# Four scatter stages, four product banks, and a last layer whose input part is worked out ahead of the attention

## What is computed

```python
x = x + einsum('bct,bcd->bdt', x, w0[subject])          # per-sequence 32x32 mix
x = x + einsum('bct,bcd->bdt', x, w1[condition])        # per-sequence 32x32 mix
x = x + attention(x, Wq, Wk, Wv, Wo, k_blocks, v_blocks, tables, lens)
x = x + (x @ W.T + (x @ A[a].T @ Bm[a].T) * scaling[a])  # a: adapter of the sequence
```

## Time and profile before

| what | us |
| --- | --- |
| median of three runs | 499.41 |
| lowest, highest | 495.37, 501.82 |
| the profiled execution | 497.69 |
| its span in the trace | 495.9 |
| TensorE busy in it | 382.6 |
| VectorE busy | 345.0 |
| ScalarE busy | 266.1 |
| GpSimd (POOL) busy | 107.7 |

### The profile page before, as it was taken

One profiled execution on the slowest core, in us unless ns is written; L12 is line 12 of the kernel. 1 busy time (PEld: TensorE's weight loads), 2 busy tenths in 40 slices (PEclk: granted clock), 3 DMA queues, 4 the chain that ended last, 5 costly groups with the idle time before them and its releaser, 6 DMA issues.

```text
span 495.9 us, 16985 instructions
## 1 busy us (share of the span) xinstructions
PE 382.6 (77%) x6190; PEld 283.8 (57%) x6190; DVE 345.0 (70%) x1017; ACT 266.1 (54%) x977; POOL 107.7 (22%) x178
## 2 busy tenths in 40 slices
PE   1753777888875006969879999999899999987996
PEld 0342534444442004757767777777777777776785
DVE  6994277898889805647656677677777777765782
ACT  3302555666665105545645766666766676654662
POOL 5300043333334620211211221211211221220000
PEclk9855798999999555799989999999999999998999
DMA  3999122222212066788877768867878969875200
GB/s 111 386 399 385 44 79 74 73 78 72 78 55 81 21 140 169 154 163 172 191 191 168 163 169 171 169 153 165 186 173 160 191 173 162 180 188 128 71 24 23
DMA packets 68866, 73.57 MB, mean 148 GB/s; under 512 B 18190, under 2 KB 65326, under 8 KB 66528
## 3 DMA queue, kind: packets, MB, share of 16 engines
q1 hardware_dynamic: 61968, 39.38, 33.9%
q0 software_dynamic: 6864, 33.72, 25.0%
HBM read 70.83 MB, written 26.21 MB: 196 GB/s over the span
## 4 chain that ended last, share of the span: by engine, by line
PE 32%; DMA 18%; ACT 9%; issue 5%; DVE 1%; SPq 1%; ACTq 0%; DVEq 0%; POOLq 0%
PE probT_bank L1123 6%; ACT rope L608 6%; PE out_bank L1147 5%; DMA kvbuf<-new_scratch,winidx 5%; PE score_banks L1084 4%; PE keys_bank L1066 3%; DMA window<-value_scratch 3%; DMA value_scratch<-kvbuf 3%; PE score_banks L1079 3%; ACT window L599 3%; PE out_bank L1134 3%; DMA out<-early 3%; DMA kvbuf<-in_kv,winidx 2%; PE out_bank L1148 2%; PE out_bank L1141 2%
## 5 line engine op out<-in xcount | busy, mean ns | idle before, releaser
L608 ACT ACTIVATE rope<-score_banks,negm 128x176 f32<-128x176 f32 x256 | 102.0, 414 | 4.2 <-DVE negm L886 4.0
L886 DVE TENSOR_REDUCE negm<-score_banks 128x2 f32<-128x352 f32 x128 | 61.0, 518 | 35.1 <-PE score_banks L1084 34.4
L896 DVE TENSOR_SCALAR rope<-rope,rinv 128x176 f32<-128x176 f32 x256 | 69.6, 314 | 4.6
L624 ACT COPY early<-probT_bank 128x128 f32<-128x128 f32 x64 | 17.0, 266 | 88.4 <-PE probT_bank L1123 88.4
L1011 PE MATMUL probT_bank<-wts,x2T 128*128 128x512 f32 x128 | 63.1, 617 | 1.8 <-DVE early L732 1.8
L433 POOL DMA_INDIRECT new_scratch<-stage,rowidx x32 | 36.5, 1142 | 111.9 <-DVE stage L757 107.0
L903 DVE COPY rope<-probT_bank 128x512 f32<-128x512 f32 x64 | 44.3, 692 | 18.6 <-PE probT_bank L1103 14.9
L608 ACT ACTIVATION_READ_ACCUMULATOR rope<-score_banks,negm 128x1 f32 x256 | 54.3, 212 | 0.0
L1123 PE MATMUL probT_bank<-rope,window 128*32 128x64 f32 x2048 | 43.8, 226 | 6.3 <-issue 3.4
L599 ACT COPY window<-keys_bank 128x352 f32<-128x352 f32 x60 | 46.7, 779 | 1.5 <-PE keys_bank L1066 1.5
L1066 PE MATMUL keys_bank<-ident,kvbuf 88*128 88x88 f32 x240 | 32.8, 262 | 16.0 <-ACT window L599 13.9
(11 more groups left out here) (179 smaller groups left out, 705.4 us busy)
## 6 DMA issues: line engine op xcount, KB each, us to landing
value_scratch<-kvbuf SPq DMA_DIRECT2D x16, 704.0 KB
window<-value_scratch SPq DMA_DIRECT2D x16, 512.0 KB, 11.6
work<-in_x SPq DMA_DIRECT2D x16, 256.0 KB, 2.7
new_scratch<-window SPq DMA_DIRECT2D x2, 2048.0 KB, 12.0
out<-early SPq DMA_DIRECT2D x32, 128.0 KB, 5.8
window<-value_scratch SPq DMA_DIRECT2D x32, 96.0 KB, 8.6
new_scratch<-kvbuf SPq DMA_DIRECT2D x1, 2048.0 KB, 14.2
wts<-in_weights SPq DMA_DIRECT2D x1, 1280.0 KB, 8.2
```

The costliest lines, as they stand in the source:

```text
L608: ins = a.activation(prob[:, par, P_AT[h]:P_AT[h] + KEYS], psS[:, h, 0:KEYS], ACT.Exp, bias=negm[:, par, h:h + 1], accum_out=sums[:, par, ...
L886: v.tensor_reduce(negm[:, par, 2 * half:2 * half + 2], psS[:, 2 * half:2 * half + 2, 0:KEYS], axis=AX_X, op=ALU.max, negate=True).then_inc ...
L896: ins = v.tensor_scalar(prob[:, par, at], prob[:, par, at], rinv[:, par, h:h + 1], None, ALU.mult)
```

## The change

Seven things change together.

1. The stage has four slots instead of two, with four semaphores; the wait for a scatter looks four tiles back instead of two.
2. `psQKV` has four banks instead of two; `qkv` may be four tiles ahead of `norm`. Two of the banks held the turned indices, so TensorE waits for their copy before `part2(0)`.
3. The work of L868 to L881 on VectorE stands ahead of the tile stage instead of behind it.
4. The last layer is linear, so it is split. In the gap TensorE makes, per tile, x2 times the weights with the identity (kept in `xres` by ScalarE) and the adapter's A times x2 (masked by VectorE into `xa2`).
5. Also in the gap, Wo is multiplied with the last layer's weights and with A (`fused`), and ScalarE keeps the products in `wo` and `woA`.
6. In the attention stage `project` uses these: two matmuls of 128 and two of 256 columns. `adapter` and `add3` are gone, `final` keeps one matmul of three, and `adapt_x2` on VectorE adds `xa2`.
7. `y_out` moves from ScalarE to VectorE, where it adds `xres`, and waits there for the store.

```diff
-        psT, psQKV, psQT = [psS[:, 2], psS[:, 3]], psP, [psK, psZ]
+        psT, psQKV, psQT = [psS[:, 2], psS[:, 3]], psP + [psS[:, 0], psS[:, 1]], [psK, psZ]
...
-        stage = sb("stage", [P, 2, 512])
+        stage = sb("stage", [P, 4, 512])
...
                 for j in range(2):
-                    scatter(2 * pair + j, j)
+                    scatter(2 * pair + j, 2 * (pair % 2) + j)
...
             def value_rows(n, j, i):
                 act.wait_ge(s["vcopy"], n + 1)
-                wait_from(act, s_scat[j], i * 16)
-                a.copy(stage[:, j, 384:512], vnew[:, j, :]).then_inc(s["vrow"], 1)
+                wait_from(act, s_scat[j], i * 8 - 8 * (j // 2))
+                a.copy(stage[:, j, 384:512], vnew[:, j % 2, :]).then_inc(s["vrow"], 1)
...
+            for u in range(2):
+                act.wait_ge(s["fused"], u + 1)
+                a.copy(woA[:, u, :], psP[u][:, 256:384])
+            act.wait_ge(s["fused"], 2)
+            for u in range(2):
+                a.copy(wo[:, u, :], psP[u][:, 0:256]).then_inc(s["fused_kept"], 1)
+            for n in range(TILES):
+                act.wait_ge(s["x2_made"], n + 1)
+                a.copy(xres[:, n, :], psS[:, n % 2, 0:256]).then_inc(s["x2_kept"], 1)
...
-            for j in range(2):
-                sumsq(j, j)
-                norm(j, j)
-            part2(0, True, True)
...
             dve.wait_ge(s["masks"], 2)
...
             ins.then_inc(s["w3_plus_one"], 1)
 
+            for j in range(2):
+                sumsq(j, j)
+                norm(j, j, j)
+            part2(0, 0, True, True)
...
-            def add3(m):
+            def y_out(m, par):
+                dve.wait_ge(s["l3"], m + 1)
+                if not (isinstance(m, int) and m < 2):
+                    dve.wait_ge(s_out[par], (m - par) * 8)
+                v.tensor_tensor(ys[:, par, :], xres[:, bass.ds(m, 1), :].rearrange("p o f -> p (o f)"), psZ[:, 0:256],
+                                ALU.add).then_inc(s["y"], 1)
...
+            def adapt_x2(m):
+                dve.wait_ge(s["xa_part"], m + 1)
+                v.tensor_tensor(xam, xam, xa2[:, bass.ds(m, 1), :].rearrange("p o n -> p (o n)"), ALU.add).then_inc(s["xam"], 1)
...
                 if par == 1 and not (known and m < 1):
                     adapt_in(m - 1)
+                if par == 0 and not (known and m < 2):
+                    y_out(m - 2, (k // 2) % 2)
                 probT_out(c, par)
+                if par == 1 and not (known and m < 1):
+                    adapt_x2(m - 1)
                 if not last:
-                    normalise(c + 1, 1 - par, 0)
-                if par == 0 and not (known and m < 1):
-                    add3(m - 1)
-                if not last:
-                    normalise(c + 1, 1 - par, 1)
+                    for half in range(2):
+                        normalise(c + 1, 1 - par, half)
...
+            for n in range(TILES):
+                dve.wait_ge(s["x2_made"], n + 1)
+                v.tensor_tensor(xa2[:, n, :].rearrange("p (b t) -> p b t", b=SPT),
+                                psS[:, 2 + n % 2, 0:P].rearrange("p (b t) -> p b t", b=SPT),
+                                spread(admask[:, n * SPT:n * SPT + SPT], 2, ROWS), ALU.mult).then_inc(s["xa2_kept"], 1)
...
             def qkv(n, j):
                 pe.wait_ge(s["xte"], n + 1)
-                wait_from(pe, s["norm"], n - 1)
-                wait_from(pe, s["vcopy"], n - 1)
+                wait_from(pe, s["norm"], n - 3)
+                wait_from(pe, s["vcopy"], n - 3)
...
+            for u in range(2):
+                for at, n, w in ((0, 256, w3T), (256, P, laT)):
+                    for f in range(2):
+                        ins = t_.matmul(psP[u][:, at:at + n], wo[:, f, P * u:P * u + P], w[:, f, :], start=(f == 0), stop=(f == 1))
+                ins.then_inc(s["fused"], 1)
+            for n in range(TILES):
+                wait_from(pe, s["x2_kept"], n - 1)
+                wait_from(pe, s["xa2_kept"], n - 1)
+                for f in range(2):
+                    t_.matmul(psS[:, 2 + n % 2, 0:P], laT[:, f, :], xres[:, n, P * f:P * f + P], start=(f == 0), stop=(f == 1))
+                for f in range(2):
+                    ins = t_.matmul(psS[:, n % 2, 0:256], xres[:, n, P * f:P * f + P], w3T[:, f, :], start=(f == 0), stop=(f == 1))
+                ins.then_inc(s["x2_made"], 1)
...
             def project(m):
                 pe.wait_ge(s["ote"], m * 2 + 2)
                 wait_from(pe, s["y"], m)
-                for f in range(2):
-                    for u in range(2):
-                        ins = t_.matmul(psZ[:, P * f:P * f + P], woT[:, u, P * f:P * f + P], oT[:, u, :],
-                                        start=(u == 0), stop=(u == 1))
+                for u in range(2):
+                    t_.matmul(psZ[:, 256:256 + P], woA[:, u, :], oT[:, u, :], start=(u == 0), stop=(u == 1))
+                for u in range(2):
+                    ins = t_.matmul(psZ[:, 0:256], oT[:, u, :], wo[:, u, :], start=(u == 0), stop=False, skip_group_check=True)
                 ins.then_inc(s["wo"], 1)
...
             def final(m):
                 pe.wait_ge(s["xam"], m + 1)
-                for f in range(2):
-                    t_.matmul(psZ[:, 0:256], x3T[:, P * f:P * f + P], w3T[:, f, :], start=(f == 0), stop=False)
-                t_.matmul(psZ[:, 0:256], xam, lbT, start=False, stop=True).then_inc(s["l3"], 1)
+                t_.matmul(psZ[:, 0:256], xam, lbT, start=False, stop=True, skip_group_check=True).then_inc(s["l3"], 1)
...
+            pe.wait_ge(s["fused_kept"], 2)
+            pe.wait_ge(s["x2_kept"], TILES)
+            pe.wait_ge(s["xa2_kept"], TILES)
             scores(0, 0, 0, 0)
```

More of the change, by code:

```diff
@@ L477, in _ @@
                     g.memset(vnat[:, :, :, 1, :], 0.0).then_inc(s["v_zero"], 1)
-            for j in range(2):
-                pool.wait_ge(s_scat[j], 16 * TILES // 2)
+            for j in range(4):
+                pool.wait_ge(s_scat[j], 16 * TILES // 4)
             for grp in range(2):
@@ L553, in qT_out, with part2 @@
                        psQT[j][:, 0:256].rearrange("p (u b t) -> p u b t", u=2, b=SPT)).then_inc(s["qte"], 1)
-            def part2(i, s1, s2, s3, s4):
+            def part2(i, q, s1, s2, s3, s4):
                 if s3:
                     for j in range(2):
-                        value_rows(i * 2 + j, j, i)
+                        value_rows(i * 2 + j, 2 * q + j, i)
                 if s2:
-                    squares(i * 2 + 2, 0)
-                    values(i * 2 + 2, 0)
+                    squares(i * 2 + 2, 2 - 2 * q)
+                    values(i * 2 + 2, 2 - 2 * q)
                 if s4:
@@ L567, in part2 @@
                     root(i * 2 + 2, 0)
-                    squares(i * 2 + 3, 1)
-                    values(i * 2 + 3, 1)
+                    squares(i * 2 + 3, 3 - 2 * q)
+                    values(i * 2 + 3, 3 - 2 * q)
                 if s1:
@@ L625, in heads_out @@
                        headsT.rearrange("p (s u t) -> p u s t", s=2, u=2)).then_inc(s["ote"], 1)
-            def y_out(m, par):
-                act.wait_ge(s["l3"], m + 1)
-                if not (isinstance(m, int) and m < 2):
-                    act.wait_ge(s_out[par], (m - par) * 8)
-                a.copy(ys[:, par, :], psZ[:, 0:256]).then_inc(s["y"], 1)
             def period(o, k):
@@ L640, in period @@
                 units = k % CPG < 2 and not (known and group >= GROUPS)
-                if par == 0 and not (known and m < 2):
-                    y_out(m - 2, (k // 2) % 2)
                 if not first:
@@ L755, in finish, with part2 @@
                 wait_from(dve, s["qt"], n - 1)
-                wait_from(dve, s_scat[j], i * 16)
-                v.tensor_tensor(stage[:, j, 0:384], rc[:, j, :], rs[:, j, :], ALU.add).then_inc(s["roped"], 1)
-            def part2(i, s2, s3):
+                wait_from(dve, s_scat[j], i * 8 - 8 * (j // 2))
+                v.tensor_tensor(stage[:, j, 0:384], rc[:, j % 2, :], rs[:, j % 2, :], ALU.add).then_inc(s["roped"], 1)
+            def part2(i, q, s2, s3):
                 if s3:
@@ L852, in _ @@
             v.tensor_copy(winidx[:].rearrange("p k g -> p (k g)"), turned_wins[0:GR]).then_inc(s["winidx"], 1)
-            for j in range(2):
-                sumsq(j, j)
-                norm(j, j)
-            part2(0, True, True)
-            part2(1, True, True)
-            base = ch.base + ch.n
-            with dve.Fori(2, PAIRS - 1) as i:
-                ch.start(base + (i - 2) * 10)
-                part2(i, True, True)
-                assert ch.n == 10
-            ch.start(base + 10 * (PAIRS - 3))
-            part2(PAIRS - 1, False, True)
             dve.wait_ge(s["masks"], 2)
@@ L881, in _ @@
             ins.then_inc(s["w3_plus_one"], 1)
+            for j in range(2):
+                sumsq(j, j)
+                norm(j, j, j)
+            part2(0, 0, True, True)
```

(24 more changed lines are left out.)

73 lines of the change are left out of this document (34 added, 39 removed).

## The result

The changed kernel takes 519.11 us (median; 517.04 to 522.40) against 500.62 for the kernel before in the same comparison: a ratio of 1.041, with an interval of 1.029 to 1.053. It is slower by about 18 us. Every ratio and interval here compares executions of both kernels in the chip's faster state alone, while a median is over all executions, so a ratio and a quotient of two medians may differ. The forecast was 504, and the range ended at 515. The profiled execution took 521.12 us, its span is 519.3.

What follows compares the result with a forecast made beforehand. VectorE and the scatter loop were taken to bound the tile stage, TensorE and window loads the attention stage. First unit +31.4 us, attention -24.9, sum +6.5 on a profiled 497.7: 504 us, range 493 to 515.

Steps and rivals of the forecast that it cites:

- The mask work, +8.4 on the path: Start of tile stage: mask work on VectorE ahead of the first sum delays everything by the full 8.4 us.
- Pairs 6.29 to 6.14: Tile stage: four stages and banks end the scatter wait, saving 0.15 us a pair; with early pairs -4.5 us together.
- The last scatter 5.80 to 1.0: End of tile stage: without mask work beside it, POOL's last scatter shortens, -4.8 us.
- The gap, +31.4: Between tile and attention stages: TensorE's new work moves the first unit from 184.72 to 216.1 us.
- Rival E: Gap: short waits for kept copies leave TensorE at its lower clock, another 40 us, 545; chance 0.05.
- Rival D: Tile stage gives nothing back: pairs stay at 6.29, last scatter stays long, 511 us; chance 0.10.
- Regular couples, 16.96 a group: Attention stage: four couples of 5.11, 4.25, 3.78 and 3.82 us, 0.7 us less a group.
- The last stretch, couple 57 to the end: End of attention stage: 39.9 us before falls to 37.6, a gain of 2.3 us.
- I add 0.3 a group: Attention stage: allowance after weighing window loads and a late store, raising a group to 17.25 us, bounds 16.6 and 17.9.
- rival B: Attention stage: the unit-fetch-gather loop decides the group, +8 us, held-up stores +2, giving 514 us; chance 0.22.
- 0.9 is left: Attention stage: window loads' lead before their unit falls from 2.35 to 0.9 us as two groups become 1.4 shorter.
- Rival C: Attention stage: couple limits too high, groups of 16.5 us, couples under 3.6, shorter gap, 491 us; chance 0.15.

Runs made afterwards that it cites:

- f2: f1 with the mask work moved on VectorE ahead of its wait for the turned indices: 498.91 us, ratio 1.005.
- g1: f3 with only the large tensor_tensor mask operation back behind the tile stage: 487.44 us, one execution.
- g2: f3 with only the large tensor_scalar mask operation back behind the tile stage: 482.69 us, one execution.
- f1: The changed kernel with four result buffers and SP issuing the odd tile's store ahead of values_out: 506.30 us, ratio 1.021.
- f3: Kernel before plus four stages and banks, masks ahead of the index wait, four result buffers, odd store first; last layer not split: 486.01 us, ratio 0.977.
- e2: The changed kernel with SP issuing the odd tile's store ahead of values_out, two result buffers kept: 507.64 us, ratio 1.032.
- f4: The kernel before with four result buffers only, SP's order unchanged: 492.26 us, ratio 0.995.

## Why the prediction was wrong, and where it was right

The prediction said 504, about no change; measured is 519, slower by 4.1%, and outside the range. By its own steps:

- **The mask work, +8.4 on the path: right**, 8.3 measured, and f2 shows the price from the other side (7.4 back when it lies in idle time).
- **Pairs 6.29 to 6.14: right.** Pairs alternate between 6.0 and 6.3 us now, and the last finish is at 164.80, forecast near 166.
- **The last scatter 5.80 to 1.0: right**, 0.98, and its reason is shown by g1 and g2. There I had weighed a rule of the Trainium skill ("SBUF — State Buffer", Who interferes with whom), by which only the tensor_scalar would hold the scatter. g1 has the tensor_tensor alone beside it, and the scatter takes 4.88 us. The measurement decides against that inferred step for this kernel. The same section of the Trainium skill also says that a VectorE operation with both inputs in SBUF, like this tensor_tensor, contends with a GpSimd instruction that reads SBUF; whether a read of the scatter is what waits here, no run shows.
- **The gap, +31.4: right**, with 213.96 for the forecast 216.1. It is 1.31 us a tile where I had 1.35. Rival E, the low clock through the gap, did not come: the granted clock was 0.96 over 168 to 216. Rival D did not come either.
- **Regular couples, 16.96 a group: right**, 5.10, 4.30, 4.03 and 3.68, 17.11 in all.
- **The last stretch, couple 57 to the end: 38.1** for 37.6.
- **"I add 0.3 a group": this step failed.** It was the allowance for held-up stores and windows, some 4 us over 14 groups. From couple 1 (220.41) to couple 57 (481.21) the kernel took 260.8 us; my sum had 69.0 + 172.5 = 241.5. The 19.3 between them are the failure. The three long couples hold 19.7, the couples behind the two store waits another 1.7 (4.09 and 4.96 for 3.68), and 14 groups of 17.11 pass 14 of 16.96 by 2.1; less the allowance of 4.1 that is 19.4.

The mechanism itself stood in the prediction: that `y_out` now puts a wait for a store's landing on VectorE, with the copy and both normalisations behind it, and that one late store alone had cost 4.79 us. What was missing was its size and what sets it. I took one wait of 4.79 in sixty-four couples as its frequency and its price, and rival B had "+2" for it. On ScalarE that wait had made its couple and the next 4.3 us longer (7.00 for 3.71 and 5.15 for 4.12); the two on VectorE, 7.05 and 6.33 us, made theirs 8.9 longer each.

What sets it is a sum of two times against a third: how late the store goes out, plus how long it takes to land, against the 16.7 to 17.0 us between a ready result and `y_out` two tiles on. In the kernel after 6.7 + 17.0 and 8.3 + 14.5 pass that. Lateness alone does not: three more odd stores went out 5.2 to 6.8 us late, landed within 7.1 us and held up nothing, like this one:

```profile
458.49 0.41 DVE L913 TENSOR_TENSOR work<-xres,out_bank 128x256 f32<-128x256 f32 x1
...
465.65 5.04 SPq L325 DMA_DIRECT2D out<-work  x2
```

In the kernel before ten of the sixteen odd stores went out over 3 us late, up to 8.3, and landed in 6.7 to 8.6 us. One was held up, because it took 13.4 us: ready at 426.8, out at 435.06, and the wait ended at 448.55:

```profile
435.06 5.41 SPq L324 DMA_DIRECT2D out<-early  x2
```

The trace of before shows where the lateness comes from, and I did not follow it: the store goes out behind `values_out`, whose wait ends with the gather, so the store is late when the gather has lost its lead. At the first wait of the kernel after the change itself had taken that lead, in the step from couple 1 to 17: the first groups run faster, the loads do not. In the kernel before the fourth `values_out` of the loop stood at 265.84, at the start of couple 15 (265.93). In the kernel after it stood at 292.49, at the start of couple 17 (292.30). Two couples of lead were gone. But in the kernel before the next one, at 284.94, was as far behind (couple 19), so what sets the two kernels apart is the two long landings as much as the lead. I priced the lead as "0.9 is left" for the unit's own wait, found no wait there, and was right about that (0.2 us in all). The price was not there but on SP's queue, one order further.

That this closes the sum: with the 16.1 us of the two store waits taken off, the span of 519.3 is 503.2, and the forecast was a span of 502.2. That it meets so closely is in part luck: couple 1 stood 2.9 us earlier than the sum had it (220.41 for 223.3), and the long couple at 246.78, which nothing in the forecast stands for, took 3.6 back. f1, in which they are taken away in fact, has a span of 502.3 and a median of 506.30. Rival B had the right sign (514) and the wrong mechanism: its gathers never made a unit wait. Rival C's couples under 3.6 did not come; the shortest regular one is 3.68. One reading of the trace was off without effect on the sum: the couples repeat within 0.02 us in five of the ten groups, not six.

So the kernel is slower for three reasons. The split costs 30.2 us of gap and gives back just 12.6 to 17.5 in the attention stage even without held-up stores (f2 and f1 against f3). The mask work stands on the path (7.4, f1 against f2). And the stores are held up (16.1 in the profile, about 10 by the ratios). Against this stand the gains in the tile stage, which f3 keeps.

What stays open: why the two stores needed 17.0 and 14.5 us to land once they were out. The DMA share in these stretches (0.80 and 0.76) is above that between them (0.69), but no run varies the load alone, and e2 changed the order and the landings together. How far f4's half per cent is the wait and how far the shift of the stores in time can't be said either.

## What to carry to other kernels

A store that is issued behind an order waiting for a load is only as early as the load: before a change that makes the consumers faster, follow each buffer's release back through the queue that issues it, and ask which orders stand ahead of it there when the loads have no lead left. Then hold that lateness plus the longest landing of the trace, not the median, against the time until the buffer is wanted: here 6.7 + 17.0 against 16.8. The order of two instructions on SP removed the waits. Work moved into an "idle" gap is free only up to the length of that gap: 32 tiles at 1.31 us are 42 us where TensorE had been idle for 21, and the attention stage gave back less than the gap took (12.6 to 17.5 for 30.2). For work that must be moved off the end of a stage, look for an earlier wait of the same engine (13.21 us in front of the indices) before putting it at the head of the next stage.

## What was not expected of the hardware

An indirect scatter on GpSimd that ran beside a long VectorE operation ended only after that operation, in both forms tried: 4.88 us beside a tensor_tensor of 4.41 us, 2.93 us beside a tensor_scalar of 2.34, 0.98 alone. The shorter VectorE operations of the tile stage (0.6 us and less) do not hold it up: the scatters there take 0.98 to 1.03 us.

One store of 128 KB landed in 16.98 us while the median of 30 was 6.9, at a DMA share of 0.80; the gather and the value windows were under way beside it. After a pause of 7.33 us on TensorE the next instructions ran at half rate (1.91 us for a form that takes 1.03), at a granted clock of 0.50, so that a wait of 7.3 us made its couple 8.45 us longer.
